# Cutting three large dtype-converting DMAs into 24 slices and issuing them at other places of an attention and feed-forward kernel

## What is computed

```python
x = x + attn(layernorm(x))            # inside attn a second layernorm, and + its input
#   q = softmax(xn Wq^T, over features of a head);  k = softmax(xn Wk^T, over tokens);  v = xn Wv^T
#   attn = k^T v per head (64 x 64);  y = q attn
h = layernorm(x)
x = x + (silu(h Wg^T / 127) * (h Wu^T / 127)) Wd^T / 127     # Wg, Wu: 3072 x 1024, Wd: 1024 x 3072, int32
```

## Time and profile before

| | |
|---|---|
| median of 3 runs | 4505.48 us (4499.14 to 5115.48) |
| the profiled execution's own time | 4496.15 us |
| its span (slowest core, core 5) | 4494.6 us |
| spans of the 8 cores | 4482.5 to 4494.6 us |
| busy share of TensorE | 81% |
| phase 1 of sequence 0 ends, by the trace | about 804 us |
| phase 2 of sequence 0, by the trace | about 810 to 1068 us |
| phase 1 of sequence 1, by the trace | about 1342 to 2022 us |

### The profile page before, as it was taken

How to read it: one execution, slowest core, us unless ns; L and a number is a source line. 1 busy time by engine, 2 the same in 40 slices (tenths; PEclk the granted TensorE clock), 3 DMA queues, 4 the chain that set the end, 5 groups by cost and what they waited for, 6 DMA issues and landing times.

```text
span 4494.6 us, 61074 instructions; the slowest of 8 cores (4482.5 to 4494.6 us)
## 1 busy us (share of the span) xinstructions
PE 3638.1 (81%) x22800; PEld 2441.8 (54%) x22800; DVE 1268.3 (28%) x3078; ACT 637.0 (14%) x1092; POOL 169.0 (4%) x295
## 2 busy tenths in 40 slices
PE   6789789116537897885354999999999999999998
PEld 4343344016433343335353677777777777777776
DVE  4312321015543213204254222222222222222222
ACT  3222221002112212212011000000000000000000
POOL 0000000000000000000000000000000000000000
PEclk6899899557558998997555999999999999999999
DMA  4111211894432112117843300000000000000000
GB/s 123 61 52 66 71 61 52 104 143 151 127 108 68 62 59 72 60 57 195 152 127 106 68 29 29 29 29 29 29 29 8 22 29 29 29 29 29 29 10 10
DMA packets 229039, 289.25 MB, mean 64 GB/s; under 512 B 83653, under 2 KB 182085, under 8 KB 226122
## 3 DMA queue, kind: packets, MB, share of 16 engines
q1 hardware_dynamic: 144666, 136.42, 11.4%
q0 software_dynamic: 33904, 136.33, 10.7%
q10 hardware_dynamic: 50176, 12.59, 1.8%
HBM read 167.86 MB, written 136.31 MB: 68 GB/s over the span
## 4 chain that ended last, share of the span: by engine, by line
PE 75%; DVE 11%; another core or an unknown queue 4%; ACT 4%; issue 3%; ACTq 2%; DMA 1%; DVEq 1%; POOL 0%; SPq 0%; POOLq 0%
PE pb L1098 30%; PE pb L1067 15%; PE pb L617 15%; PE pb L555 9%; DVE h_st L912 3%; ACTq L94 2%; PE pb L773 2%; PE pb L825 1%; DVE n_t L520 1%; ACT h1n_t L932 1%; DVE hnT_lo_st L843 1%; DVE xnT_lo L528 1%; PE pb L367 1%; ACT hnT_hi_st L838 1%
## 5 line engine op out<-in xcount | busy, mean ns | idle before, releaser
L1098 PE MATMUL pb<-hnT_hi_b,wgT 128*128 128x256 bf16 x3072 | 838.4, 273 | 10.3 <-DMA s_hnT_lo<-hnT_lo_st 10.3
L1098 PE MATMUL pb<-hnT_lo_b,wgT 128*128 128x256 bf16 x3072 | 838.3, 273 | 0.0
L1098 PE MATMUL pb<-hnT_hi_b,wuT 128*128 128x256 bf16 x3072 | 838.3, 273 | 0.0
L1098 PE MATMUL pb<-hnT_lo_b,wuT 128*128 128x256 bf16 x3072 | 838.1, 273 | 0.0
L1111 DVE SCALAR_TENSOR_TENSOR g_t<-pb,g_t 128x256 f32<-128x256 f32 x384 | 162.8, 424 | 1446.2 <-ACT g_t L1107 1424.3
L1067 PE MATMUL pb<-wdT_t,hmT_hi 128*128 128x512 bf16 x1536 | 457.6, 380 | 7.1 <-DVE hmT_hi L1117 6.9
L1067 PE MATMUL pb<-wdT_t,hmT_lo 128*128 128x512 bf16 x1536 | 457.7, 380 | 0.0
L1107 ACT ACTIVATE g_t<-pb 128x256 f32<-128x256 f32 x384 | 147.5, 384 | 1859.1 <-PE pb L1098 1859.0
L1098 PEld LDWEIGHTS pb<-hnT_hi_b,wgT 128*128 128x128 bf16 x3072 | 300.9, 98 | 85.1 <-issue 11.0
L1098 PEld LDWEIGHTS pb<-hnT_lo_b,wgT 128*128 128x128 bf16 x3072 | 300.9, 98 | 74.4 <-issue 0.3
L555 PE MATMUL pb<-wvT_hi,xnT_hi 128*128 128x512 bf16 x512 | 192.6, 465 | 176.1 <-DVE v_stg L585 169.7
(11 more groups left out here) (146 smaller groups left out, 4230.9 us busy)
## 6 DMA issues: line engine op xcount, KB each, us to landing
x_r<-x SPq DMA_DIRECT2D x32, 512.0 KB, 4.3
s_r<-r_r POOLq DMA_DIRECT2D x32, 512.0 KB, 5.0
s_v<-v_stg POOLq DMA_DIRECT2D x32, 512.0 KB, 2.9
s_qT<-qT_stg POOLq DMA_DIRECT2D x64, 256.0 KB, 2.6
s_kT<-kT_stg POOLq DMA_DIRECT2D x64, 256.0 KB, 2.6
kTe<-s_kT SPq DMA_DIRECT2D x16, 1024.0 KB, 5.9
v_p<-s_v SPq DMA_DIRECT2D x16, 1024.0 KB, 6.9
qT_c<-s_qT SPq DMA_DIRECT2D x32, 512.0 KB, 7.3
```

The source lines that it names most:

```text
L1098: hc=hc, bsl=bsl, st=st, sp=sp: e.matmul(pb[bnk][:, 0:256], wtt[:, d, hc * 128:(hc + 1) * 128], xt.ap()[:, bsl, d, :], start=st, stop=sp),
```

## The change

The three DMAs become 24 slices of a contiguous 1.5 MB of int32 each (eight of gate, eight of up, eight of down, in this order). `pump_cast` issues the next slice, if one is left. It is called once per pair in phase 2 (of both sequences), and once per chunk in phase 1 of sequence 1. The call after phase 1 of sequence 0 is gone; before the FFN's early loads `emit_casts` issues whatever is left. The loads of FFN weights wait for all eight slices of their matrix instead of one DMA.

```diff
-    m_cast = {}
+    m_cast = {"g": [], "u": [], "d": []}
+    cast_slices = []
+    for j in range(8):
+        cast_slices.append(("g", s_wg[j * 384:(j + 1) * 384, :],
+                            wg_i[j * 384:(j + 1) * 384, :]))
...
+    def pump_cast():
+        if cast_slices:
+            w, dst, srcq = cast_slices.pop(0)
+            m_cast[w].append(P.dma("gpsimd", dst, srcq))
 
     def emit_casts():
-        m_cast["g"] = P.dma("gpsimd", s_wg[:, :], wg_i[:, :])
-        m_cast["u"] = P.dma("gpsimd", s_wu[:, :], wu_i[:, :])
-        m_cast["d"] = P.dma("gpsimd", s_wd[:, :], wd_i[:, :])
+        while cast_slices:
+            pump_cast()
...
@@ phase1, end of the loop over chunks
             if c % 4 == 3 and (c + 1) * 128 <= T:
                 kblock(c // 4)
+            if s == 1:
+                pump_cast()
...
@@ the stages
             phase2_prefetch(int(nm[-1]))
-            if nm == "p1s0":
-                emit_casts()
             P.fence(pre)
         elif nm == "p2s1" and upto == "all":
             pre = P.fence_markers()
+            emit_casts()
             emit_early_ffn_loads()
```

More of the change, by code:

```diff
@@ L294, in build @@
     m_bcolf = colize(bcol_f[:], pw_f.ap()[:, 1, :], m_b_row, 7)
-    m_cast = {}
+    m_cast = {"g": [], "u": [], "d": []}
[3 more added lines that the diff above has]
+                            wg_i[j * 384:(j + 1) * 384, :]))
+    for j in range(8):
+        cast_slices.append(("u", s_wu[j * 384:(j + 1) * 384, :],
+                            wu_i[j * 384:(j + 1) * 384, :]))
+    for j in range(8):
+        cast_slices.append(("d", s_wd[j * 128:(j + 1) * 128, :],
+                            wd_i[j * 128:(j + 1) * 128, :]))
+    def pump_cast():
+        if cast_slices:
+            w, dst, srcq = cast_slices.pop(0)
+            m_cast[w].append(P.dma("gpsimd", dst, srcq))
     def emit_casts():
-        m_cast["g"] = P.dma("gpsimd", s_wg[:, :], wg_i[:, :])
-        m_cast["u"] = P.dma("gpsimd", s_wu[:, :], wu_i[:, :])
-        m_cast["d"] = P.dma("gpsimd", s_wd[:, :], wd_i[:, :])
+        while cast_slices:
+            pump_cast()
     pw_free = [[m_gcol], [m_bcolf], [], []]
@@ L951, in emit_early_ffn_loads @@
                     "scalar", wgT[:, d, rows], s_wg[rows, d * 128:(d + 1) * 128],
-                    waits=deps + [m_cast["g"]], transpose=True)
+                    waits=deps + m_cast["g"], transpose=True)
                 mw[("u", d, half)] = P.dma(
                     "scalar", wuT[:, d, rows], s_wu[rows, d * 128:(d + 1) * 128],
-                    waits=[m_cast["u"]] + deps, transpose=True)
+                    waits=m_cast["u"] + deps, transpose=True)
         early_ffn["m"] = mw
@@ L1011, in build @@
             "sync", wdT_t[:, hc, :], s_wd[0:D, hc * 128:(hc + 1) * 128],
-            waits=[m_cast["d"]], transpose=True)
+            waits=m_cast["d"], transpose=True)
     hb_res = [Res(), Res()]
```

## The result

| | before | changed |
|---|---|---|
| profiled execution | 4496.15 us | 4390.43 us |
| spans of the 8 cores | 4482.5 to 4494.6 us | 4368.7 to 4388.8 us |
| median of 10 runs | 4744.42 us | 4393.15 us |
| lowest | 4494.77 us | 4385.49 us |

The change makes the kernel faster: the ratio is 0.9758, with a 95% interval of 0.9744 to 0.9773. In some executions of either kernel the cores of one die or both run some per cent longer at a lower clock; the ratio is taken without them, and they put the median of before at 4744.42 us here. The forecast was 4396 us. The mean span of the eight cores went from 4488.8 to 4376.1 us, by 112.7 us; the slowest core, now another one, by 105.8 us.

What follows compares the result with a forecast made beforehand. TensorE's 171.4 us wait for `v_p` behind the conversions was taken as the bound. -111.6 + 7.2 = -104.4 us from 4496.15 gave 4391.8 us, plus 4 us for the median: 4396 us, range 4362 to 4430 us.

Steps and rivals of the forecast that it cites:

- The bound and the turn-taking: Phase 2 of sequence 0: TensorE waits 171.4 us for `v_p`, whose load gets one 512-byte packet per conversion packet.
- The form of the wait: Phase 2 of sequence 0: one wait of L773 for `v_p` of 57 to 65 us, until the burst ends.
- rival B: Phase 2 of sequence 0: loads get through between the slices, up to 35 us more gained, 4370 us; chance 0.12.
- The burst, -111.6 us: Phase 2 of sequence 0: gate's eight slices go out together, so L773 starts at 875.5 instead of 987.1 us.
- Phase 1 of sequence 1 at nothing: Sixteen slices there cost 0 us, hidden by some 30 us of slack; 22 us kept for the range.
- rival C: Phase 1 of sequence 1 pays 10.7 us per slice, 171 us in all, giving 4567 us; chance 0.05.
- Room for slices: Phase 1 of sequence 1: slices ask for 115 us of DMA time in 685 us with a DMA share of 0.19.
- The 24th slice, +7.2 us: End of phase 1 of sequence 1: a slice before the last store of v makes it land 7.2 us later.
- The sum: -104.4 us forecast: Whole kernel: -111.6 + 7.2 us, taking the profiled execution from 4496.15 to 4391.8 us.
- Rival A: Conversions: a piece costs 4.8 us whatever its size, so gate needs 76.6 us; 4418 us, chance 0.11.
- Rival D: Phase 2 of sequence 0: the slices do spread and the stall vanishes (-171 us), 4336 us; chance 0.03.
- The rule of 9 to 17 descriptors in a packet: DMA queues: by it the `v_p` load would need 8 to 14 turns, 29 to 50 us; one row per turn was kept.

Runs made afterwards that it cites:

- casts_behind_fence: Kernel before with the three whole DMAs issued behind the fence instead of ahead of it, nothing sliced or moved to another phase: ratio 1.0004.
- paced_by_pair: Changed kernel with each slice of phase 2 waiting for its pair's last matmul: ratio 0.9683 to the kernel before, 4361 us.
- sliced_in_place: Kernel before with the 24 slices issued in one go where the three DMAs stood, ahead of the fence: ratio 1.0003.
- whole_moved: Kernel before, uncut: gate behind phase 2's fence (sequence 0), up and down after chunks 1 and 9 of phase 1 (sequence 1); ratio 0.9736, 4384.9 us.

## What of the prediction held and what failed, point by point

The time came out as forecast, and the step that should have given it did not happen as described. The step that failed is "the load of `v_p` goes out with the fence, at the same moment as the burst", with what follows from it: that the load gets 16 of its 128 packets per engine during the burst and "must wait for the end of the burst again", so that L773 starts once, at 875.5 us. In its place pair 0 ran at 816.17 us, before most of the burst, and it was pair 1 that waited, twice: 18.8 us for its k and 35.5 us for its v on the slowest core. That the total fits all the same is in part luck, since two other errors went the other way (see the burst, below).

- **The bound and the turn-taking: right.** Packets 1 to 1 in three kernels (464, 857, 260), one long stall for as long as conversions are queued, and no effect of cutting alone. One reading of the page was too wide: slices 8 and 9 are not the only place with full DMA engines and an idle TensorE. The loads of the FFN's weights are a second one, with TensorE busy 29 of 110 us.
- **The form of the wait: wrong, as said.** The load and the burst were issued 1 us apart (v at 806.25, slices from 807.23 us on core 5), but the first row of v moved 1.65 us after its issue and the first piece of gate 5.2 us after its own. In the 4.5 us between the two (807.90 to 812.39 us) 1629 of 2048 rows got started. I had a head start in rival B, priced at two to three pairs; it was one. casts_behind_fence shows that a head start over three matrices is paid back in full: the conversions end 10.3 us later, and the second pair's v comes behind them. No run takes the head start alone out of the changed kernel.
- **The burst, -111.6 us: -116.4 us measured on core 5** (L789 of the second pair starts at 881.78 us, against 998.19 us). Three errors make up the 4.8 us. Pair 0's run inside the burst took away the 11.1 us that lie between the two pairs' products in the kernel before. The last piece of gate ended at 874.6 instead of 871.0 us, 67.4 us behind the first issue instead of 63.3: +3.6 us. And from there to the product it took 7.1 us instead of 4.5: +2.7 us. The slices landed 7.3 us apart, where 7.2 were expected.
- **Phase 1 of sequence 1 at nothing: right.** 675.3 against 674.8 us by landmarks, with TensorE busy 568 us in both. The slack of some 30 us is that of the load shown in the earlier trace rows; six of the 16 have 117 us or more. The 22 us that I held back for instruction fetches and table loads did not come, nor did rival C.
- **Room for slices: over-sized.** I took 16 x 7.2 = 115 us of DMA time. The DMA share went from 0.18 to 0.28, which is some 68 us for the 15 slices of that stretch; by the DMA records their pieces take 4.2 us a slice. A slice by itself moves faster than one in a burst.
- **The 24th slice, +7.2 us: right in sign, +5.1 us** (8.6 less 3.5), for the same reason.
- **The sum: -104.4 us forecast.** The slowest core gave -105.8, the mean core -112.7, and the ratio 2.4%, some 109 us. That the slowest core comes so near is in part luck, too: it lost less than the mean core.
- **Rival A (a piece costs a turn whatever its size): false.** Pieces of 24.6 KB took 3.4 us and those of 32.8 KB 4.7 us, eight slices about as long as one whole matrix, and 24 slices in one go as long as three.
- **Rival D (slices that spread)** was no case of this kernel, but paced_by_pair shows what it would bring: half of what was left (0.9758 to 0.9683, where 0.9614 is to be had), not all.
- **The rule of 9 to 17 descriptors in a packet** (the Trainium skill, page "DMA: Bandwidth & Descriptors", section "Queues, rings and completion order"): the trace of the changed kernel bears it out no more than that of before did. Each turn took one row, 857 against 857 in sliced_in_place, and pair 0's early run came from the head start, not from several rows per turn.

What stays open is who shares the limit of a long conversion. The runs only hint at it. In whole_moved, counted from each core's own first instruction, cores 1, 2, 5 and 6 begin the conversion of up 1 to 8 us ahead of cores 0, 3, 4 and 7, and their first pieces take 2.4 to 3.1 us (medians over the 16 engines); the first pieces of the later four take 5.0 to 5.6 us. At the end it is the other way round: the last pieces of cores 0 and 3 take 3.4 and 3.6 us, those of 1 and 2 still 4.7 us. That looks like cores sharing in pairs (0 and 1, 2 and 3, 4 and 5, 6 and 7), each slowed by its neighbour. The Trainium skill, page "HBM Reference", section "Specifications (TRN2)", says that two cores share the bandwidth of a memory domain and that some 358 GB/s are left for each; here a core wrote 106 GB/s (before) and 116 GB/s (changed) during the conversions and read twice that, since int32 becomes bf16, together 318 to 348 GB/s. The long conversions agree with that figure. A slice by itself does not keep to it: on core 5 ten of the 15 slices in phase 1 of sequence 1 wrote their 0.79 MB in 4.0 to 4.6 us, which with the reads is 510 to 590 GB/s. That fits a limit that a core meets only while its neighbour converts as well, but no run had one core of a pair convert alone, so it isn't shown.

## What to carry to other kernels

A DMA with long contiguous pieces starves one with many short rows on other queues of the same engines: they take turns by piece, not by byte. Cutting such a DMA up does not help as long as the cuts are queued back to back; putting it beside a stage whose loads have rows of several KB and whose buffers have time to spare does. A slice needs some 7 us of that time. A whole matrix needs up to 56 us, so it has to meet those loads and stores that have it, here the ones ahead of a `kblock` (117 us); the 35 us of the other loads would not have covered the 47 us that one load took. And a call written inside a loop spreads nothing if its engine has no other work and no wait in that loop.

## What was not expected of the hardware

- A single slice of 0.8 MB on a quiet queue ran at 1.83 us for a piece of 24.6 KB (median of the DMA records), one in the burst at 3.4 us, and a whole matrix took 4.7 us for 32.8 KB on 16 engines and 2.5 us on 8. In the burst, from 850 to 870 us of core 1, the engines were full and moved 116 GB/s, counted by the bytes written:

```profile
850.00:870.00 20.00, 0.00 (x0) 0.00 (x0) 0.16 (x1) 0.00 (x0) 0.00 (x0) 0.50 0.98 116
```

- A converting DMA of POOL starts late. On core 5 of the changed kernel its first piece moves 5.2 us after its issue, a plain load of SP 1.65 us after its own; in the kernel before it was 2.7 us (804.66 to 807.32 us). With issues 1 us apart (806.25 and 807.23 us) the load gets 4.5 us alone, and most of its 1 MB goes through in them.
